# Cross attention on one core: V projected first, one head per period, K and V in one-bank blocks

## The chip, the cores and the metric
The kernel runs on one core of one Trainium2 chip. Its time is the device time of one launch in microseconds; one launch computes all 16 batches. All arithmetic is float32, and most matmuls split each operand into a high and a low part (float32r), so that one product becomes three: high x high, high x low, low x high.

## The reference
B = 16 batches, S = 100 rows of x with H = 640 features, 8 heads of D = 80, an encoder sequence of 718 rows (KEYS) with C = 384 features, and T = 4 further rows ca. Cut to what matters:

```python
query, keyt, valt = x @ Wq, enc @ Wk, enc @ Wv
hs = mha(query, keyt, valt)                        # softmax(Q K^T / sqrt(80)) V, 8 heads
ca_q1 = einsum('btc,th->bch', ca, Wq_ca)[:, indices, :]   # 100 of 384 rows
ca_hs1 = mha(ca_q1, x, x)
ca_hs2 = mha(ca_hs1 @ Wq, ca @ Wk_ca, ca @ Wv_ca)  # over 4 keys
out = (hs + ca_hs2) @ Wout + b_out + x
```

## The kernel before
`prepare` makes what depends on weights and x alone (Q of all batches, the small tables of the second attention) and writes it to DRAM. `attend` has the main stage, a loop over batches, and then the output projection over tiles of 128 rows. This case is about `attend`.

Each engine has its own program, an order written out by hand (`batch(i)` in each engine's block), and semaphores between them. Nothing is scheduled at run time: an instruction that waits holds everything behind it on its engine. Names of one batch's steps:

- `keys(b, f)`, line 887: one of five 128-feature tiles of K^T = Wk^T enc^T over all 718 columns, as two halves of 360 in two PSUM banks (`psS`, shared with the scores). ScalarE copies the high part (`k_high`, L1131), VectorE makes the low part (`k_low`, L1346).
- `lift` on SP, L674 and L677: DMAs that restack K^T from tiles of 128 features to heads of 80 rows, in `kstack`, 120 rows for two copies and the low parts, with four slots for heads.
- `scores(i, h)`, L864: four matmuls into `psS`. VectorE takes the row maximum (`rowmax`, L1322), ScalarE the exponential with its sum (`expo`, L1114), VectorE normalises (`norm`, L1327 and L1329).
- `turn(i, h)`, L901: six transpositions of P into `psT`; ScalarE `pt_high` (L1120), VectorE `pt_low` (L1335).
- `context(i, u)`, L918: U = enc^T P^T for four heads at once, 400 columns, one of three 128-feature tiles for each half of the heads; ScalarE `u_high` (L1149), VectorE `u_low` (L1351). It needs enc in its natural layout (`encN`), which is loaded and split besides `encT`: ScalarE L1143, GpSimd L812.
- `values(i, half)`, L941, L947, L948: Wv^T U per head, with the second attention's last product in the same accumulation.
- The second attention: `b2_scores` (L961), `b2_less_max` (VectorE, L1358 and L1360), `b2_exp`, `b2_norm` (VectorE, L1366, L1368, L1370), `b2_turn` (L971), `b2_values` (L984), `b2_scores2`, `b2_less_max2`, `b2_exp2`, `b2_norm2` (L1403 to L1407), and `b2_turn2` (L1007), one transposition of P2x per batch. GpSimd prepares its operands (`spread_g` L779 to L788, `split_x`).

Steps of three batches overlap: the contexts 2 to 5 and the values of a batch run in the next one, and the first three K tiles of the next batch run in this one. The output projection (`tile`, L1022, thirty matmuls of 320 columns) needs Wout split; ScalarE copies it (`wo_high`, L1181), GpSimd makes its low parts (L835).

Of the kernel before, what the change touches and what calls it, by code (L numbers as in the profile page):

```python
# [13 lines left out]
HEADS = 8  # L14
# [13 lines left out]
KT = 6  # L28
# [4 lines left out]
GT = 4 * S  # L33
STK = 3 * D // 2
# [45 lines left out]
def build(nc, x, xT, encT, encN, caT, asel, Wq, WqT, Wk, Wv, WqcaBD, Wkca, Wvca, Wout, bout, out):  # L80
# [6 lines left out]
    with ExitStack() as keep:  # L87
# [7 lines left out]
        Wo_s = [t[:, 0:FT * H].rearrange("p (c n) -> p c n", c=FT) for t in (wk_keep, eT_keep)]  # L95
# [3 lines left out]
        attend(nc, Wk_s, Wv_s, Wo_s, eT_s, ident, headmask, x, encT, encN, asel, Wout, bout,  # L99
# [392 lines left out]
def attend(nc, Wk_s, Wv_s, Wo_s, eT_s, ident, headmask, x, encT, encN, asel, Wout, bout,  # L492
# [6 lines left out]
    with ExitStack() as ctx:  # L499
# [9 lines left out]
        PRING = 3  # L509
        PARTS = CT  # L510
        KQ = KT // PARTS
        encT_raw, enc_raw = sb("encT_raw", [128, CT * KEYS]), sb("enc_raw", [128, KT * C])
        rawT = encT_raw[:, :].rearrange("p (c k) -> p c k", c=CT)
        rawN = enc_raw[0:KP, :].rearrange("p (k c) -> p k c", k=KT)
        eT = eT_s
        eN = pair("encN", [KP, KT, C])
        kT = [pair(f"kT{j}", [128, KEYS]) for j in range(2)]

        kst = sb("kstack", [STK, 2, SLOTS, KEYS], F32R)
        P = [sb(f"probs{j}", [128, KPAD]) for j in range(PRING)]  # L520
        PT = pair("PT", [KP, KT, R])
        UT = sb("UT", [128, CT, 4, 2, S], F32R)

        qst = pair("qstack", [STK, HEADS, S])
        hs = sb("hs", [D, RH])
        negmax, total, inv = sb("negmax", [S, HEADS]), sb("total", [S, HEADS]), sb("inv", [S, HEADS])

        xr, xs = sb("x_raw", [S, H]), pair("x", [S, H])
# [3 lines left out]
        v2 = sb("v2bd", [ST, H], F32R)  # L532
        Ms = sb("Min", [D, 2, HEADS, HEADS, T], F32R)
        P1 = sb("P1", [S, HEADS, S])
# [3 lines left out]
        P2T = sb("P2T", [ST, S], F32R)  # L538
        st1 = sb("st1", [S, 3, HEADS])
        st2 = sb("st2", [S, 3, HEADS])  # L540


        hs1T = [[PT[p][0:D, 0:4, (7 - half) * S:(8 - half) * S] for half in range(2)] for p in range(2)]

        psS = [ctx.enter_context(nc.psum_tensor(f"psS{j}", [128, 2, 512], F32)) for j in range(2)]
        psT = ctx.enter_context(nc.psum_tensor("psT", [128, 2, 512], F32))

        psB = ctx.enter_context(nc.psum_tensor("psB", [128, 2, 512], F32))


        loads = "rawT rawN qin gin ain xin v2in min woin0 woin1 bias hsout"

        products_done = "scores pt u kp hsp b2s b2t b2pv b2c b2t2 cmm"

        exps_and_highs = "exp pthi uhi khi hscopy b2exp p1hi hs1hi b2exp2 p2hi encThi encNhi wohi chi"

# [17 lines left out]
        score_slot = [0, 1, 1, 0, 0, 1, 0, 0]  # L574
# [1012 lines left out]
```

## Time and profile before
| | |
|---|---|
| three runs | 1098.77, 1101.1, 1110.14 us |
| median | 1101.1 us |
| profiled execution, first to last instruction | 1101.6 us |
| mean granted TensorE clock | 0.963 |
| first b2_turn2 to the last, 15 batches | 177.7 to 1019.8 us |

The profiled execution is given by its span alone; no other time of it is recorded. Read the table with the rows further down: times in them are microseconds from the start of the span, a duration in a group row is the mean of one instruction in ns, and TensorE's instructions overlap, so that the distance between two starts tells what one costs the stream.

### The profile page before, as it was taken

How to read it: one execution, taken by the hardware profiler on the slowest of the kernel's cores; microseconds unless marked ns; L12 is line 12 of the kernel's file. 1: busy time of each engine (PE TensorE's matmuls, PEld its weight loads, DVE VectorE, ACT ScalarE, POOL GpSimd, SP SyncE). 2: the span in 40 equal slices, each digit the busy share in tenths (PEclk: the TensorE clock that was granted, in tenths of full speed). 3: DMA queues.
4: the chain of work that ended last, by engine and by line, in shares of the span. 5: the costliest groups of instructions: out<-in, count | busy, mean ns of one | idle time of the engine just before them, and what ended most of it. 6: DMA issues, size and time to landing. Idle time of an engine off the chain costs nothing.

```text
span 1101.6 us, 21261 instructions
## 1 busy us (share of the span) xinstructions
PE 1036.2 (94%) x7192; PEld 1011.9 (92%) x7192; DVE 668.4 (61%) x1138; ACT 490.6 (45%) x889; POOL 280.9 (26%) x208
## 2 busy tenths in 40 slices
PE   6998759999989899999999998999999999998998
PEld 5997749999989899999999998999999999898997
DVE  4444356676756656576656674667675676666344
ACT  4443243635454535354545453455544454445110
POOL 0000132323231322323233323142433151415000
PEclk9899779999999999899999998999998999999999
DMA  8676786767887969596969694869695969697255
GB/s 303 219 204 154 166 173 153 182 163 187 170 171 148 196 133 202 119 211 139 193 142 212 138 196 112 207 148 208 145 198 112 206 152 195 142 200 184 66 172 160
DMA packets 155050, 189.51 MB, mean 172 GB/s; under 512 B 78416, under 2 KB 108112, under 8 KB 155024
## 3 DMA queue, kind: packets, MB, share of 16 engines
q1 hardware_dynamic: 151696, 181.63, 72.3%
q10 hardware_dynamic: 3328, 7.54, 2.1%
q8 instruction: 16, 0.26, 0.1%
q14 instruction: 10, 0.08, 0.0%
HBM read 81.15 MB, written 19.74 MB: 92 GB/s over the span
## 4 chain that ended last, share of the span: by engine, by line
PE 70%; DMA 11%; SPq 4%; DVE 2%; ACT 1%; issue 1%; POOL 0%; DVEq 0%; ACTq 0%; POOLq 0%
PE psB L918 23%; PE psS L887 20%; DMA kstack<-kT_l 10%; PE psS L864 6%; PE psT L901 5%; PE psS L1022 4%; PE psT L941 4%; PE psT L947 2%; SPq L677 2%; PE psB L984 2%; SPq L674 1%; PE psB L1002 1%; DVE kT_l L1346 1%; PE psB L996 1%; PE psT L948 1%
## 5 line engine op out<-in xcount | busy, mean ns | idle before, releaser
L887 PE MATMUL psS<-encT_keep,Wk_keep 128*128 128x360 f32 x1440 | 264.1, 338 | 5.9 <-PEq L173 5.3
L887 PEld LDWEIGHTS psS<-encT_keep,Wk_keep 128*128 128x128 f32 x1440 | 247.4, 196 | 6.7 <-issue 5.3
L918 PE MATMUL psB<-PT_h,encN_h 120*128 120x400 f32 x576 | 203.7, 354 | 0.2 <-POOL encN_l L812 0.2
L918 PE MATMUL psB<-PT_l,encN_h 120*128 120x400 f32 x576 | 199.4, 346 | 0.0
L918 PE MATMUL psB<-PT_h,encN_l 120*128 120x400 f32 x576 | 198.5, 345 | 0.0
L1114 ACT ACTIVATE probs<-psS,negmax 100x718 f32<-100x718 f32 x128 | 110.4, 863 | 169.9 <-DVE negmax L1322 146.6
L1346 DVE TENSOR_TENSOR kT_l<-psS,kT_h 128x718 fp32r<-128x718 f32 x80 | 72.4, 905 | 112.0 <-ACT kT_h L1131 111.9
L1131 ACT ACTIVATE kT_h<-psS 128x718 fp32r<-128x718 f32 x80 | 61.7, 771 | 146.9 <-PE psS L887 137.0
L804 POOL TENSOR_TENSOR encT_keep<-encT_raw,encT_keep 128x718 fp32r<-128x718 f32 x45 | 79.4, 1763 | 181.5 <-ACT encT_keep L1137 179.1
L864 PE MATMUL psS<-kstack,qstack_h 120*100 120x360 f32 x256 | 90.7, 354 | 32.8 <-DMA kstack<-kT_l 27.0
L812 POOL TENSOR_TENSOR encN_l<-enc_raw,encN_h 120x768 fp32r<-120x768 f32 x48 | 90.7, 1889 | 116.3 <-ACT encN_h L1143 115.0
L1322 DVE TENSOR_REDUCE negmax<-psS 100x1 f32<-100x720 f32 x128 | 113.6, 897 | 2.6 <-PE psS L864 2.5
L918 PEld LDWEIGHTS psB<-PT_h,encN_h 120*128 120x128 f32 x576 | 109.2, 190 | 1.5 <-POOL encN_l L812 0.8
L1335 DVE TENSOR_TENSOR PT_l<-psT,PT_h 120x600 fp32r<-120x600 f32 x128 | 99.7, 779 | 16.0 <-ACT PT_h L1120 10.8
L918 PEld LDWEIGHTS psB<-PT_l,encN_h 120*128 120x128 f32 x576 | 109.3, 190 | 0.0
L918 PEld LDWEIGHTS psB<-PT_h,encN_l 120*128 120x128 f32 x576 | 108.9, 189 | 0.0
L1351 DVE TENSOR_TENSOR UT<-psB,UT 128x400 fp32r<-128x400 f32 x96 | 55.0, 573 | 84.1 <-ACT UT L1149 84.1
L1329 DVE TENSOR_SCALAR probs<-probs,inv 100x718 f32<-100x718 f32 x128 | 103.0, 805 | 4.5
L901 PE MATMUL psT<-ident,probs 100*120 100x100 f32 x768 | 87.8, 250 | 8.6 <-DVE PT_l L1335 7.2
L1149 ACT ACTIVATE UT<-psB 128x400 fp32r<-128x400 f32 x96 | 48.4, 504 | 97.5 <-PE psB L918 97.3
L901 PEld LDWEIGHTS psT<-ident,probs 100*120 100x120 f32 x768 | 78.0, 137 | 15.0 <-issue 11.1
L795 POOL CAST x_h<-x_raw 100x640 fp32r<-100x640 f32 x16 | 14.2, 890 | 290.5 <-DMA x_raw<-in_x_dram 290.5
(143 smaller groups left out, 1868.4 us busy)
## 6 DMA issues: line engine op xcount, KB each, us to landing
kstack<-kT_h SPq DMA_DIRECT2D x64, 448.8 KB
kstack<-kT_l SPq DMA_DIRECT2D x192, 112.2 KB
enc_raw<-in_encN_dram SPq DMA_DIRECT2D x16, 1080.0 KB, 10.9
encT_raw<-in_encT_dram SPq DMA_DIRECT2D x15, 1077.0 KB, 8.5
kstack<-kT_h SPq DMA_DIRECT2D x32, 359.0 KB
kstack<-kT_h SPq DMA_DIRECT2D x32, 269.2 KB
kstack<-kT_h SPq DMA_DIRECT2D x32, 179.5 KB, 4.1
xT_raw<-in_xT_dram SPq DMA_DIRECT2D x4, 1000.0 KB, 7.8
```

The lines of the kernel that those rows point to most:

```text
L804: nc.gpsimd.tensor_tensor(eT[1][:, c, :], rawT[:, c, :], eT[0][:, c, :], ALU.subtract).then_inc(s["encT"], 1)
L812: nc.gpsimd.tensor_tensor(eN[1][:, ks, :], rawN[:, ks, :], eN[0][:, ks, :], ALU.subtract).then_inc(s["encN"], 1)
L864: mm = pe.matmul(psS[score_slot[h]][0:S, half, 0:HALF], qst[p][:, h, :], kst[:, p, h % SLOTS, k0:k0 + HALF], start=(p == 0), stop=(p == 1))
L887: mm = pe.matmul(keys_in(f, first)[:, half, 0:HALF], w[:, c, f * 128:(f + 1) * 128], e[:, c, k0:k0 + HALF], start=(j == 0), stop=(j == 3 * ...
L901: mm = pe.transpose(psT[0:KP, k // 3, (k % 3) * S:(k % 3 + 1) * S], P[h % PRING][0:S, k * KP:(k + 1) * KP], ident[0:S, 0:S])
L918: mm = pe.matmul(psB[:, 1, 0:RH], e[:, k, c * 128:(c + 1) * 128], a[:, k, half * RH:(half + 1) * RH], start=(j == 0), stop=(j == 3 * KT - 1))
L1114: nc.scalar.activation(halves(P[h % PRING][0:S, 0:KEYS]), without_overlap(psS[score_slot[h]], S), ACT.Exp, bias=negmax[:, h:h + 1], accum_ ...
L1131: nc.scalar.activation(halves(kT[f % 2][0][:, :]), without_overlap(keys_in(f, first), 128), ACT.Copy).then_inc(s["khi"], 1)
L1322: nc.vector.tensor_reduce(negmax[:, h:h + 1], tile_in(h), AX.XY, ALU.max, negate=True).then_inc(s["negmax"], 1)
L1329: nc.vector.tensor_scalar(P[h % PRING][0:S, 0:KEYS], P[h % PRING][0:S, 0:KEYS], inv[:, h:h + 1], None, ALU.mult).then_inc(s["norm"], 1)
L1335: nc.vector.tensor_tensor(o[1], psT[0:KP, :, 0:3 * S].rearrange("p a (k n) -> p a k n", k=3), o[0], ALU.subtract).then_inc(s["ptlo"], 1)
L1346: nc.vector.tensor_tensor(halves(kT[f % 2][1][:, :]), without_overlap(keys_in(f, first), 128), halves(kT[f % 2][0][:, :]), ALU.subtract).t ...
```

## The change
Three things go together.

1. V = enc Wv is made first, in twelve blocks ("v", columns, k) of up to 120 keys x 320 features, nine matmuls each, from `encT` and `Wv`. Then `values(i, j, h)` forms V^T P^T per head: six matmuls of 200 columns (high and low part of P^T side by side), six of 100, one for the second attention. `context` and its evictions go, and so do the load and the split of `encN`.
2. K is made in ten half tiles ("k", f, half), one bank each. K and V blocks, 22 a batch, alternate between the two banks of `psK`; block n waits for the low part of block n - 2. Scores have `psS` for themselves, one buffer: scores of a head wait for the exponential of the head before.
3. Each engine's batch is laid out in eight periods, one per head: scores, a block, the turn of the head before, a block, the values of the head before that, and often a third block. `OWN` and `NEXT` say which blocks a period has. The second attention runs one batch ahead, spread over the periods. `encT`, the values' small operands and PT have two buffers, and the loop body holds two batches.

On SP, q comes in two halves of heads and hs is stored in quarters. In the last batch Wout is loaded at the start, copied by ScalarE at the end of period 5, and its low parts are made by GpSimd after the last K block. The diff, cut to its core, SP first, then GpSimd's last batch, TensorE, ScalarE (exponential, period 0, end of period 5), VectorE (periods 0 to 4):

```diff
+BLOCKS = (("k", 0, 0), ("k", 0, 1), ("v", 0, 0),
+          ("k", 1, 0), ("k", 1, 1), ("v", 0, 1),
+          ("v", 0, 2), ("v", 0, 3), ("v", 0, 4),
+          ("k", 2, 0), ("k", 2, 1), ("v", 0, 5),
+          ("k", 3, 0), ("k", 3, 1), ("v", 1, 0),
+          ("v", 1, 1), ("v", 1, 2),
+          ("k", 4, 0), ("k", 4, 1), ("v", 1, 3),
+          ("v", 1, 4), ("v", 1, 5))
+NB = len(BLOCKS)
+AT = {what: n for n, what in enumerate(BLOCKS)}
+
+
+OWN = ((6, 7, 8), (9, 10, 11), (12, 13, 14), (15, 16), (17, 18, 19), (20, 21), (), ())
+NEXT = ((), (), (), (), (), (), (0, 1, 2), (3, 4, 5))
...
+                def batch(i, j, first=False, last=False):
+                    if not last:
+                        load_ga(i + 1)
+                        load_encT(i + 1)
+                        load_x(i + 1)
+                    else:
+                        load_wo()
+                    lift(i, 2)
                     if not first:
+                        store_hs(i - 1, 3)
                     lift(i, 3)
+                    if not last:
+                        load_q(i + 1, 0)
+                    else:
+                        for k in range(2):
+                            sp.wait_ge(s[f"hsout{k}"], 32 * (B - 1))
+                    store_hs(i, 0)
+                    if not last:
+                        load_m(i + 1)
                     lift(i, 4)
+                    if not last:
+                        load_v2(i + 1, 1 - j)
+                    else:
+                        for t in range(2):
+                            sp.wait_ge(s["wolo"], t + 1)
+                            load_tile(t)
+                    store_hs(i, 1)
                     if not last:
                         lift(i + 1, 0)
+                        load_q(i + 1, 1)
                         lift(i + 1, 1)
+                    store_hs(i, 2)
...
+                pool.wait_ge(s["bp"], NB * (B - 1) + AT["k", 4, 1] + 1)
...
+                def projected(b, j, n):
+
+                    what, f, half = BLOCKS[n]
+                    if n == 0:
+                        wait_pos(pe, s["encT"], CT * b)
+                    wait_pos(pe, s["blo"], NB * b + n - 1)
+                    m = 0
+                    if what == "k":
...
+                    else:
+                        cols, k = f, half
+                        for c in range(CT):
+                            for e, w in products(eT[j], Wv_s):
+                                mm = pe.matmul(psK[0:tiles_of(k), n % 2, 0:VH], e[:, c, k * KP:k * KP + tiles_of(k)],
+                                               w[:, c, cols * VH:(cols + 1) * VH], start=(m == 0), stop=(m == 3 * CT - 1))
+                                m += 1
+                    mm.then_inc(s["bp"], 1)
...
+                def values(i, j, h):
+
+                    pe.wait_ge(s["ptlo"], HEADS * i + h + 1)
+                    if h == 0:
...
+                    def high(k):
+                        n = tiles_of(k)
+                        return pe.matmul(both, V[0][0:n, k, hh], pt[0:n, k, :, :].rearrange("p a n -> p (a n)"),
+                                         start=(k == 0), stop=(k == KT - 1))
+
+                    def low(k):
+                        n = tiles_of(k)
+                        pe.matmul(o, V[1][0:n, k, hh], pt[0:n, k, 0, :], start=False, stop=False)
+
+                    for k in range(KT - 1):
+                        high(k)
+                        low(k)
+                    low(KT - 1)
+                    pe.matmul(o, v2[j][:, hh], P2T[j][:, :], start=False, stop=False)
+                    high(KT - 1).then_inc(s["pv"], 1)
...
+                    scores(i, 0)
+                    block(0, 0)
                     if not first:
+                        turn(i - 1, 7)
+                    block(0, 1)
                     if not first:
+                        values(i - 1, 1 - j, 6)
+                    b2_turn2(i)
+                    block(0, 2)
+
+                    scores(i, 1)
+                    block(1, 0)
+                    turn(i, 0)
+                    block(1, 1)
+                    if not first:
+                        values(i - 1, 1 - j, 7)
+                    block(1, 2)
+                    if not last:
+                        b2_scores(i + 1, 0)
+
                     scores(i, 2)
+                    block(2, 0)
+                    turn(i, 1)
+                    block(2, 1)
+                    values(i, j, 0)
+                    if not last:
+                        b2_scores(i + 1, 1)
+                    block(2, 2)
+
                     scores(i, 3)
+                    block(3, 0)
                     turn(i, 2)
+                    values(i, j, 1)
+                    block(3, 1)
+
                     scores(i, 4)
+                    if not last:
+                        b2_turn(i + 1, 0)
+                    block(4, 0)
+                    turn(i, 3)
+                    block(4, 1)
+                    values(i, j, 2)
+                    block(4, 2)
+
                     scores(i, 5)
+                    if not last:
+                        b2_turn(i + 1, 1)
+                    block(5, 0)
+                    turn(i, 4)
+                    values(i, j, 3)
+                    if not last:
+                        b2_values(i + 1, 0)
+                    block(5, 1)
+
                     scores(i, 6)
+                    block(6, 0)
+                    turn(i, 5)
+                    block(6, 1)
+                    if last:
+                        tile(0)
+                    values(i, j, 4)
+                    if not last:
+                        b2_values(i + 1, 1)
+                    block(6, 2)
+
                     scores(i, 7)
+                    block(7, 0)
                     turn(i, 6)
+                    if not last:
+                        b2_scores2(i + 1)
+                    block(7, 1)
+                    values(i, j, 5)
+                    block(7, 2)
+
+                b2_scores(0, 0)
+                projected(0, 0, 0)
                 b2_scores(0, 1)
+                projected(0, 0, 1)
+                projected(0, 0, 2)
+                projected(0, 0, 3)
+                b2_turn(0, 0)
+                projected(0, 0, 4)
+                b2_turn(0, 1)
+                projected(0, 0, 5)
+                b2_values(0, 0)
+                projected(0, 0, 6)
+                b2_values(0, 1)
+                projected(0, 0, 7)
+                projected(0, 0, 8)
+                b2_scores2(0)
...
+                def expo(i, h):
                     act.wait_ge(s["negmax"], HEADS * i + h + 1)
+                    wait_pos(act, s["pt"], HEADS * i + h - 1)
...
+                    expo(i, 0)
+                    block(0, 0)
                     if not first:
+                        pt_high(i - 1, 7)
+                    block(0, 1)
+                    b2_exp2(i)
+                    block(0, 2)
+                    b2_pt2_high(i, j)
...
+                    if not last:
+                        b2_hs_high(i + 1, 0)
+                    else:
+                        for c in range(FT):
+                            wo_high(c)
+                        tile_high(0)
...
+                    rowmax(i, 0)
+                    block(0, 0)
+                    norm(i, 0)
                     if not first:
+                        pt_low(i - 1, 7)
+                    block(0, 1)
+                    b2_norm2(i)
+                    block(0, 2)
+                    b2_pt2_low(i, j)
+
+                    rowmax(i, 1)
+                    block(1, 0)
+                    norm(i, 1)
+                    pt_low(i, 0)
+                    block(1, 1)
                     if not first:
+                        hs_add(i - 1, 3)
+                    block(1, 2)
+                    if not last:
+                        b2_less_max(i + 1, 0)
+
                     rowmax(i, 2)
+                    block(2, 0)
+                    norm(i, 2)
+                    pt_low(i, 1)
+                    block(2, 1)
+                    if not last:
+                        b2_less_max(i + 1, 1)
+                    block(2, 2)
+
                     rowmax(i, 3)
+                    block(3, 0)
                     norm(i, 3)
                     pt_low(i, 2)
+                    if not last:
+                        b2_norm(i + 1)
+                    hs_add(i, 0)
+                    block(3, 1)
+
                     rowmax(i, 4)
+                    block(4, 0)
+                    if not last:
+                        b2_pt_low(i + 1, 0)
+                    norm(i, 4)
+                    pt_low(i, 3)
+                    block(4, 1)
+                    block(4, 2)
```

## Rows read from the trace of the kernel before
**Rows 1.** The page, first part: busy us, share of the span, instructions.
```profile
PE 1036.2 (94%) x7192; PEld 1011.9 (92%) x7192; DVE 668.4 (61%) x1138; ACT 490.6 (45%) x889; POOL 280.9 (26%) x208
```
**Rows 2.** Windows cut at b2_turn2: busy by engine, granted clock, DMA share, GB/s.
```profile
109.70:177.70 68.00, 49.62 (x269) 46.54 (x270) 32.09 (x58) 23.73 (x43) 18.81 (x15) 0.76 0.74 156
...
572.00:625.20 53.20, 53.19 (x387) 52.34 (x386) 36.29 (x64) 27.03 (x51) 17.93 (x12) 1.00 0.77 176
625.20:686.70 61.50, 57.99 (x390) 56.80 (x388) 36.22 (x64) 27.51 (x51) 16.80 (x12) 0.92 0.75 156
...
907.10:963.10 56.00, 53.37 (x388) 52.65 (x387) 36.40 (x64) 27.34 (x51) 17.66 (x12) 1.00 0.81 170
...
1019.80:1101.60 81.80, 75.27 (x516) 74.19 (x513) 35.46 (x47) 12.42 (x21) 0.00 (x0) 1.00 0.43 133
```
**Rows 3.** The waits: engine, line, for whom, us in total, times, longest.
```profile
PE psS L864 <- DMA kstack<-kT_l: 27.0, 13, 4.4
```
**Rows 4.** TensorE's timeline in one batch and in the tail: start, us, form.
```profile
501.59 3.19 PE L887 MATMUL psS<-encT_keep,Wk_keep 128*128 128x360 f32 x18
504.61 0.68 PE L901 MATMUL psT<-ident,probs 100*120 100x100 f32 x6
505.07 0.39 PE L864 MATMUL psS<-kstack,qstack_h 120*100 120x360 f32 x1
...
518.36 0.35 PE L918 MATMUL psB<-PT_h,encN_h 120*128 120x400 f32 x1
...
521.63 0.33 PE L864 MATMUL psS<-kstack,qstack_h 120*100 120x360 f32 x1
...
529.87 0.46 PE L941 MATMUL psT<-UT,Wv_h 128*80 128x200 f32 x3
530.17 0.35 PE L947 MATMUL psT<-UT,Wv_l 128*80 128x100 f32 x3
530.36 0.24 PE L948 MATMUL psT<-P2T,v2bd 96*80 96x100 f32 x1
...
1025.52 0.31 PE L1022 MATMUL psS<-Wk_keep,kT_h 128*128 128x320 f32 x1
...
1029.94 0.35 PE L918 MATMUL psB<-PT_h,encN_h 120*128 120x400 f32 x1
```
**Rows 5.** Timeline of VectorE and ScalarE, a row maximum and what follows.
```profile
522.86 0.90 DVE L1322 TENSOR_REDUCE negmax<-psS 100x1 f32<-100x720 f32 x1
...
523.87 0.86 ACT L1114 ACTIVATE probs<-psS,negmax 100x718 f32<-100x718 f32 x1 [1.53 <-DVE negmax L1322]
...
524.88 0.87 ACT L1159 ACTIVATE P<-P 100x800 f32<-100x800 f32 x1
```
**Rows 6.** Groups by form: times | busy us, mean ns | idle before, released by.
```profile
L1329 DVE TENSOR_SCALAR probs<-probs,inv 100x718 f32<-100x718 f32 x128 | 103.0, 805 | 4.5
L1335 DVE TENSOR_TENSOR PT_l<-psT,PT_h 120x600 fp32r<-120x600 f32 x128 | 99.7, 779 | 16.0 <-ACT PT_h L1120 10.8
L1346 DVE TENSOR_TENSOR kT_l<-psS,kT_h 128x718 fp32r<-128x718 f32 x80 | 72.4, 905 | 112.0 <-ACT kT_h L1131 111.9
L1351 DVE TENSOR_TENSOR UT<-psB,UT 128x400 fp32r<-128x400 f32 x96 | 55.0, 573 | 84.1 <-ACT UT L1149 84.1
L1149 ACT ACTIVATE UT<-psB 128x400 fp32r<-128x400 f32 x96 | 48.4, 504 | 97.5 <-PE psB L918 97.3
L1370 DVE TENSOR_TENSOR P<-P,st 100x800 f32<-100x800 f32 x16 | 17.2, 1074 | 0.6
L1366 DVE TENSOR_REDUCE st<-P 100x8 f32<-100x800 f32 x16 | 15.7, 979 | 0.0
```
**Rows 7.** GpSimd: the last step of its first work, and the low parts of Wout.
```profile
114.28 0.39 POOL L788 TENSOR_TENSOR a<-a_raw,a 32x100 fp32r<-32x100 f32 x1
...
L835 POOL TENSOR_TENSOR encT_keep<-encT_raw,Wk_keep 128x640 fp32r<-128x640 f32 x5 | 8.2, 1638 | 11.0 <-ACT Wk_keep L1181 10.7
```
**Rows 8.** The lifts' issues on SP, from issue to landing.
```profile
DMA to landing us min/median/max: 2.9/4.3/8.5
```

More of the change, by code:

```diff
@@ L954, in b2_scores @@
+                def b2_scores(i, half):
                     if half == 0:
@@ new lines, in _ @@
+                b2_values(0, 1)
+                projected(0, 0, 7)
+                projected(0, 0, 8)
+                b2_scores2(0)
+                batch(0, 0, first=True)
+                with pe.Fori(0, (B - 2) // 2) as r:
+                    batch(2 * r + 1, 1)
+                    batch(2 * r + 2, 0)
+                batch(B - 1, 1, last=True)
+                tile(1)
+                turn(B - 1, 7)
+                values(B - 1, 1, 6)
+                tile(2)
+                values(B - 1, 1, 7)
@@ new lines, in _ @@
+                batch(0, 0, first=True)
+                with act.Fori(0, (B - 2) // 2) as r:
+                    batch(2 * r + 1, 1)
+                    batch(2 * r + 2, 0)
+                batch(B - 1, 1, last=True)
+                pt_high(B - 1, 7)
+                tile_high(2)
+                store(0)
+                load_x(2)
+                hs_copy(B - 1, 3)
+                for t in range(1, TILES):
+                    if t + 2 < TILES:
+                        tile_high(t + 2)
+                    store(t)
+                    if t + 2 < TILES:
+                        load_x(t + 2)
@@ L1506, in _ @@
+                    if not last:
+                        b2_less_max2(i + 1)
+                    hs_add(i, 2)
+                    block(7, 2)
+                for j in range(2):
+                    nc.vector.memset(P[j][:, KEYS:KPAD], 0.0).then_inc(s["ready"], 1)
                 b2_less_max(0, 0)
-                rowmax(0, 0)
+                low(0, 0)
                 b2_less_max(0, 1)
-                rowmax(0, 1)
-                batch(0, first=True)
-                with dve.Fori(1, B - 1) as i:
-                    batch(i)
@@ new lines, in _ @@
+                b2_pt_low(0, 0)
+                low(0, 4)
+                b2_pt_low(0, 1)
+                low(0, 5)
+                b2_hs_low(0, 0)
+                low(0, 6)
+                b2_hs_low(0, 1)
+                low(0, 7)
+                low(0, 8)
+                b2_less_max2(0)
+                batch(0, 0, first=True)
+                with dve.Fori(0, (B - 2) // 2) as r:
+                    batch(2 * r + 1, 1)
+                    batch(2 * r + 2, 0)
+                batch(B - 1, 1, last=True)
```

1014 lines of the change are left out of this document (401 added, 613 removed).

## The prediction
> **What bounds the kernel now.** I read the busy shares first: TensorE is busy 94% of the 1101.6 us, VectorE 61% [rows 1]. Then the main stage batch by batch, cut at the one transposition of P2 that every batch has. The windows show two kinds of batch: undisturbed ones of 53.2 us at full clock, in which TensorE is never idle, and ones of 56 to 61.5 us [rows 2]. What makes the difference is in the list of waits: TensorE waited 27.0 us in 13 places for a kstack transfer [rows 3], and after most of these the granted clock was at its lower level (1.2 of 2.4 GHz) for a while. In [rows 2] the batch of 61.5 us at clock 0.92 lost 61.5 x 0.08 = 4.9 us to that, the one of 56.0 us at clock 1.00 nothing; over the nine of fifteen such windows with a wait of over 1 us the loss, added up in this way, is 20.7 us, 2.3 on average. So the bound is TensorE's stream (15 batches of 53.2 = 798 us of the 842 us from the first such transposition to the last), and what can be won in the loop is 44 us of waits and low clock. The first batch is far worse: 68.0 us at clock 0.76 for less than a batch of work [rows 2]. The profiled execution's span, 1101.6 us, is 0.5 us over the median of the runs (1101.1), so I add up spans and take the sum as the median.
>
> **The TensorE work hardly changes.** Costs are distances between starts, since recorded matmuls overlap [rows 4]. A K tile of 18 matmuls of 360 columns takes 504.61 - 501.59 = 3.02 us (0.168 each), a transposed head 0.46, a context group of 18 x 400 columns 521.63 - 518.36 = 3.27, thirty matmuls of 320 columns 4.42 (0.147 each). In the values, three of 200 columns take 0.30 and three of 100 columns 0.19. Removed per batch: six context groups, 19.6 us, and both values steps, 8 heads x 0.56 = 4.5 us; together 24.1. Added: twelve V blocks of nine matmuls of 320 columns, 12 x 1.32 = 15.9 us, and eight heads of 6 x 0.10 + 6 x 0.063 + 0.07 = 1.05, 8.4 us; together 24.3. The alternation of 200 and 100 columns is in no row; from below the pair costs its columns (0.125), from above 0.172 (0.10 and the small matmul's 0.07): -0.2 to +0.06 us a head. I take 0.163, since both kinds are in the rows next to each other. K as ten half blocks of 1.51 us costs what five tiles did. The batch stays at 53.6 us of TensorE. The gain of the product order itself is nothing; all depends on the waits.
>
> **A rule that speaks against it.** The rows show a 360-column matmul every 0.168 us, 0.150 of which are its columns at 2.4 GHz, so a 128-column weight load is nearly hidden [rows 4]. The Trainium skill, TensorE: Matmul & The Clock Gate, sections LDWEIGHTS and The mechanism, has a load cost its columns at 1.2 GHz and overlap a running matmul only in another row group. The rows disagree with that. By it the change would load 21,280 columns of weights a batch in place of 18,304, some 2.5 us more; I leave it to the last rival.
>
> **What the new order asks of VectorE.** Each batch is now eight periods, and each period's order on VectorE is: row maximum, low part of block A, normalise, low part of P^T of the head before, low part of block B, something of the second attention, block C. Low A stands behind ScalarE's exponential of the same head, which stands behind the row maximum. From [rows 5]: maximum at 522.86, exponential at 523.87 (1.01 later), the next ScalarE instruction at 524.88 (1.01 later); with the block's high part, 0.504 for 400 columns and some 0.45 for 320 to 360 [rows 6], low A starts 2.5 us after the maximum started, and VectorE, busy for 0.82 of it, is idle 1.7 us in each of eight periods. That idle time is hidden while TensorE's period is longer than VectorE's. K and V evictions cost VectorE more too: ten of 360 and twelve of 320 columns. Between 573 ns at 400 and 905 at 718 columns [rows 6] the slope is 1.04 ns a column, so 0.53 and 0.49, or 0.45 and 0.41 where the next one follows (records overlap by 0.08): 9.4 us against 5 x 0.83 + 6 x 0.49 = 7.1 before. Four additions of hs in place of two cost about 0.3 more. Removed are the load and the splits of enc in its other layout, on ScalarE and GpSimd; nothing on the path of [rows 2]'s full-clock batches waited for them, so I count them at nothing.
>
> TensorE's periods by these prices: 0: 6.3; 1: 6.8; 2: 6.8; 3: 4.9; 4: 7.0; 5: 6.2; 6: 7.5; 7: 8.0 us. Periods 3 and 0 are where TensorE asks for something that the second attention makes on VectorE.
> *Wait A*, b2_turn of the next batch right after scores(4): from the start of scores(3) VectorE needs 0.66 (scores) + 0.2 (a matmul's end lies 501.59 + 3.19 - 504.61 = 0.17 behind the next start [rows 4]) + 2.5 + 0.41 (low A) + 0.93 (reciprocal and scaling, 0.805 on average [rows 6]) + 0.70 (P^T low) + 2.2 (b2_norm: 0.98 + 0.2 + 1.07 [rows 6]) = 7.6 us. TensorE is there after 0.66 + 1.32 + 0.56 + 1.05 + 1.32 + 0.66 = 5.6. It waits 2.0. VectorE also enters period 3 late: both b2_less_max passes (1.1 us each, two passes of 400 columns) stand at the end of periods 1 and 2, the first after a block low part that itself ends some 1.1 us into the next period. Followed through that is 0.9 us, so A is 2.0 to 3.0; I take 2.9. Queued behind b2_turn on TensorE are block 17, the turn of head 3 and everything else.
> *Wait B*, b2_turn2 in period 0: 0.66 + 0.2 + 2.5 + 0.41 + 0.93 + 0.70 + 0.41 (low B) + 0.75 (b2_norm2, three dependent short steps) = 6.6 us, against 0.66 + 1.32 + 0.56 + 1.32 + 1.05 = 4.9: 1.7 us.
> Elsewhere every block has its low part out of the way 1.4 us or more before its bank is wanted, and scores, turns and values want results of a period earlier.
>
> **The lifts.** Their number and bytes are the same. A lift lands 4.3 us after issue (median; 8.5 at most [rows 8]), and now each K tile is finished one and a half to two periods, about 9 us, before the first head that needs it. SP's queue gets four more q loads and two more hs stores; they stand between lifts, each in a gap of a period. The 27 us of waits and their low clock go. At scores(4) a landing can be up to 1 us late, in front of wait A, which covers it.
>
> **Clock.** A batch with waits lost 0 to 5.4 us before, 2.3 on average; now each batch has 4.6 us of waits in two places. I take 2.3, with 0 and 5.4 as ends.
> Batch period: 53.6 + 2.9 + 1.7 + 2.3 = 60.5 us, against (1019.8 - 177.7) / 15 = 56.1.
>
> **Ramp and tail.** TensorE's first instruction is now b2_scores, behind GpSimd's split of a, which ended at 114.67 [rows 7]; before, K started at 109.7. Then 12.9 us of blocks, 4.3 of the second attention, 2.7 for the cold clock, 2.5 waiting for b2_norm: scores(0,0) at 137.2, and after the chain of period 0 scores(0,1) at about 142.1, with no lift waits. From scores(15,1): 38.6 us of periods, of which nothing of the next batch is part; tiles 50.9; head 6, 7 and the last turn 2.7; the drain 4.6. In the last batch the split of Wout is queued on ScalarE at the end of period 5, and GpSimd's five low parts follow it at 1.64 us [rows 7] and 0.15 between them: 9 us, which the first output tile in period 6 waits out. I put that at 9.2 and 2.0 for the clock behind it. Together 108.0.
> Sum: 142.1 + 15 x 60.5 + 108.0 = 1157.6, say **1158 us**.
>
> **The rivals.**
> *TensorE-bound, faster.* The waits A and B don't form, the lift waits are gone, P is 54.2, the tail wait half hidden: 142.1 + 813 + 102 = 1057. For it: VectorE's busy time is only some 38 us a batch (36.3 to 37.2 busy before [rows 2], plus 2.6, less overlap), so on average there is room. Against: both waits come out of a chain in one queue, and no average fills it. It needs VectorE to be 2 us faster over one period; its longest single step there, the scaling at 0.805 [rows 6], would have to vanish, and more. Chance 0.12.
> *Waits without the clock.* A at 2.0, B 1.7, full clock after them as after the one of the 56.0 us batch, Wout hidden: P = 57.3, 142.1 + 859.5 + 97 = 1098.6: no change. Chance 0.14.
> *Low clock after every wait, slower still.* Its place is behind b2_turn in period 4 and behind b2_turn2: if TensorE's clock falls to 1.2 GHz at both in every batch, the loss is that of the worst window, 5.4 us, and P = 63.6: 1204. Chance 0.10.
> *Narrow weight loads not hidden.* If each of the twelve alternating matmuls of a head paid its load, about 0.06, it would be 0.76 a head, 6 us a batch, of which 1.5 only shorten A and B: 1158 + 15 x 4.5 = 1226. The skill's rule above has less, 2.5 us a batch: near 1195. Rows 4 speak against both. Chance 0.03.
> *It doesn't do what it says*: the lifts still hold scores because DMA queues are as full as before (0.77 to 0.81 busy [rows 2]). Each would cost 1 us where no other wait covers it; this only adds to my forecast, inside its range.
>
> **How the numbers follow.** The forecast itself has 0.61. The range reaches from 1095, just under the no-change case, to 1200: below it lies the faster rival, above it part of the last two. Faster by over 1% (under 1090) 0.13, within 1% 0.12, slower 0.75. One per cent, 11 us, is about what runs of this kernel can tell (they lie 11 us apart).
>
> **What would show it.** Each batch should have two idle places on TensorE: before the transpositions of P (b2_turn, released by VectorE's P normalisation), 2 to 3 us, and before the one of P2x, 1.7 us. kstack should be gone from the list of waits. Batches should be near 60 us, evenly, with clock 0.93 to 1.0; V blocks 1.32 us apart per nine. VectorE's low part of block A should start 2.5 us after the row maximum. The first output tile should wait some 9 us for GpSimd's split of Wout. I am wrong if TensorE reaches b2_turn later than VectorE's normalisation ends, or if the clock stays up after waits of 2 to 3 us.

## The result, and the profile after
| | before | after |
|---|---|---|
| median of four runs each, us | 1099.93 (1098.42 to 1110.14) | 1178.65 (1176.03 to 1179.59) |
| profiled execution: span | 1101.6 | 1174.0 |
| mean granted TensorE clock | 0.963 | 0.954 |

The ratio is 1.0675, 95% interval 1.0616 to 1.0733 (the two medians alone would give 1.072): the change makes the kernel slower by 6.8%. The forecast was 1158 us, range 1095 to 1200. Ratios, here and in the experiments, leave out slow runs, in which the granted clock was lower: some of the kernel before, more than 1.5% above its fastest run on the same chip, and one of experiment 5, 1673.9 us at clock 0.555.

The first part of the page after and its row of the granted clock, to be set against [rows 1]:

```profile
span 1174.0 us, 23696 instructions
## 1 busy us (share of the span) xinstructions
PE 1048.1 (89%) x7960; PEld 1023.8 (87%) x7960; DVE 695.9 (59%) x1345; ACT 490.1 (42%) x1049; POOL 179.6 (15%) x160
...
PEclk9997889899999999999989999999999999999799
```

TensorE is busy 12 us longer than before while the span grew by 72: 60 of the 72 are idle time of TensorE. The windows of after, cut as in [rows 2] at the one transposition of P2x that every batch has (columns: window, its length, busy by engine, clock, DMA share, GB/s). A common batch, one with a loop end in it, the only one at full clock, and the tail:

```profile
443.30:503.20 59.90, 55.44 (x434) 54.47 (x434) 38.14 (x77) 27.16 (x60) 10.90 (x9) 0.97 0.55 140
747.00:810.20 63.20, 57.14 (x433) 55.85 (x434) 38.31 (x77) 27.38 (x60) 10.93 (x10) 0.95 0.54 137
992.50:1050.70 58.20, 53.82 (x434) 52.87 (x435) 38.06 (x77) 26.93 (x60) 10.86 (x9) 1.00 0.58 147
1050.70:1174.00 123.30, 101.40 (x710) 99.86 (x710) 56.29 (x88) 30.80 (x60) 8.15 (x5) 0.91 0.51 146
```

The third row is the one to read: at full clock a batch has 53.8 us of TensorE work, 0.6 more than one before ([rows 2]: 53.20), and still takes 58.2. Where the 4.4 us are, and what else waits, is in the list of waits of after (for whom, us in total, times, longest), which answers to [rows 3]:

```profile
PE psB L942 <- DVE P L1381: 49.8, 16, 3.3
...
PE psB L978 <- DVE P2x L1418: 21.8, 16, 4.8
...
PE psS L858 <- issue: 11.5, 6, 2.3
...
PE psB L932 <- POOL a L799: 10.4, 1, 10.4
...
PE psK L996 <- POOL Wk_keep L843: 8.6, 1, 8.6
```

kstack, 27.0 us before, is gone from it: the high part of a lift lands 3.0 us after its issue (median, 3.3 at most), against 4.3 and 8.5 [rows 8]. L942 is b2_turn in period 4 (wait A), L978 is b2_turn2 in period 0 (wait B). L858 is the first scores of every second batch. L996 is the first output tile. L932 is b2_scores, TensorE's first instruction here.

Wait A on TensorE, first the start of scores(3) and then b2_turn (start, duration, form, idle time before):

```profile
458.29 0.32 PE L858 MATMUL psS<-kstack,qstack_h 120*100 120x360 f32 x1
...
467.18 0.55 PE L942 MATMUL psB<-ident,P 100*100 100x100 f32 x4 [3.18 <-DVE P L1381]
```

The chain in front of it on VectorE, from the row maximum of head 3 to the end of b2_norm:

```profile
459.57 0.90 DVE L1330 TENSOR_REDUCE negmax<-psS 100x1 f32<-100x720 f32 x1
461.81 0.49 DVE L1362 TENSOR_TENSOR V_l<-psK,V_h 120x320 fp32r<-120x320 f32 x1 [1.35 <-ACT V_h L1145]
462.22 0.15 DVE L1335 RECIPROCAL inv<-total 100x1 f32<-100x1 f32 x1
462.41 0.59 DVE L1337 TENSOR_SCALAR probs<-probs,inv 100x718 f32<-100x718 f32 x1
462.92 0.78 DVE L1343 TENSOR_TENSOR PT<-psT,PT 120x600 fp32r<-120x600 f32 x1
463.61 0.97 DVE L1377 TENSOR_REDUCE st<-P 100x8 f32<-100x800 f32 x1
464.62 0.20 DVE L1379 RECIPROCAL st<-st 100x8 f32<-100x8 f32 x1
464.86 2.27 DVE L1381 TENSOR_TENSOR P<-P,st 100x800 f32<-100x800 f32 x1
```

and GpSimd's row in the same time:

```profile
464.58 1.70 POOL L814 TENSOR_TENSOR encT_keep<-encT_raw,encT_keep 128x718 fp32r<-128x718 f32 x1 [5.38 <-ACT encT_keep L1151]
```

TensorE reaches b2_turn at 467.18 - 3.18 = 464.00, 5.71 us after scores(3) started (forecast 5.6). VectorE is 0.39 us into the first of b2_norm's three steps then. The last of them took 2.27 us where 1.07 was allowed: over all sixteen the median is 2272 ns and the least 991. (The 1074 ns of [rows 6] is itself a mean: before, the median was 992 and the longest 1467.) GpSimd's low part of encT had started 0.28 us earlier and ended at 466.28. If VectorE's step could do its work only from there, it would end at 466.28 + 0.99 = 467.27; it ended at 467.13. The Trainium skill says as much (SBUF — State Buffer, Who interferes with whom): a VectorE instruction with both inputs in SBUF and a GpSimd instruction that reads SBUF share a port pair, and the second fully blocks until the first is through. P and st both lie in SBUF, and GpSimd's step reads SBUF; the trace agrees to 0.14 us.

What the clock did behind this wait is in four windows: three in a row from the end of wait A, and one from the end of wait B (shown below) in the same batch:

```profile
467.18:469.00 1.82, 1.82 (x12) 1.82 (x13) 1.43 (x3) 0.35 (x1) 0.00 (x0) 0.86 0.45 111
469.00:471.00 2.00, 2.00 (x11) 1.92 (x10) 0.71 (x2) 1.67 (x5) 0.00 (x0) 0.50 0.29 82
471.00:473.00 2.00, 2.00 (x14) 1.99 (x12) 1.66 (x4) 0.58 (x2) 0.00 (x0) 0.77 0.00 0
...
503.15:506.00 2.85, 2.85 (x19) 2.85 (x20) 0.66 (x2) 0.57 (x2) 0.43 (x1) 1.00 0.24 45
```

Behind wait A TensorE works at 1.2 GHz for a while, which costs 0.14 x 1.82 + 0.50 x 2.00 + 0.23 x 2.00 = 1.7 us; behind wait B it stays at 2.4 GHz.

Wait B, and the wait at the end of the loop body:

```profile
503.15 0.29 PE L978 MATMUL psB<-ident,P2x 100*96 100x100 f32 x1 [1.28 <-DVE P2x L1418]
```

```profile
437.08 0.40 PE L858 MATMUL psS<-kstack,qstack_h 120*100 120x360 f32 x1 [1.65 <-issue]
```

"issue" means that nothing the profile shows held TensorE. It occurs six times, at each return to the start of the loop body, which now holds two batches. The queue that brings instructions moved 76 packets:

```profile
q8 instruction: 76, 1.25, 0.4%
```

against 16 before. In the tail two output tiles stand still for long, the first for GpSimd's Wout, the third for the low part of its hs tile:

```profile
1091.57 0.60 PE L996 MATMUL psK<-encT_keep,kT_h 128*128 128x320 f32 x1 [8.63 <-POOL Wk_keep L843]
```

```profile
1113.44 0.64 PE L996 MATMUL psK<-encT_keep,kT_h 128*128 128x320 f32 x1 [5.00 <-DVE kT_l L1432]
```

### The profile page after: what moved, and what is told of

It reads as the page before. It is cut to its first block, busy times and chain, and to the rows that moved or that the text cites. A ratio compares the mean times of both kernels' runs of the same rounds, so it can differ in the third digit from the quotient of the medians.

```text
span 1174.0 us, 23696 instructions
## 1 busy us (share of the span) xinstructions
PE 1048.1 (89%) x7960; PEld 1023.8 (87%) x7960; DVE 695.9 (59%) x1345; ACT 490.1 (42%) x1049; POOL 179.6 (15%) x160
## 3 DMA queue, kind: packets, MB, share of 16 engines
q8 instruction: 76, 1.25, 0.4%
## 4 chain that ended last, share of the span: by engine, by line
PE 60%; DVE 18%; issue 8%; ACT 3%; POOL 1%; DMA 1%; ACTq 0%; DVEq 0%; SPq 0%; POOLq 0%
PE psK L873 18%; PE psK L880 14%; PE psH L910 5%; PE psS L858 4%; PE psT L890 4%; DVE negmax L1330 3%; DVE P L1381 3%; PE psK L996 3%; DVE PT L1343 3%; PE psB L955 2%; DVE V_l L1362 2%; PE psH L915 2%; PE psS L996 2%; ACT V_h L1145 2%; PE psB L942 2%
## 5 line engine op out<-in xcount | busy, mean ns | idle before, releaser
L910 PE MATMUL psH<-PT,V_h 120*80 120x200 f32 (+1 forms) x768 | 155.2, 279 | 0.0
L873 PE MATMUL psK<-encT_keep,Wk_keep 128*128 128x360 f32 x720 | 148.2, 354 | 0.0
L880 PE MATMUL psK<-Wv_h,encT_odd 128*120 128x320 f32 (+1 forms) x576 | 147.3, 318 | 0.0
L873 PE MATMUL psK<-encT_odd,Wk_keep 128*128 128x360 f32 x720 | 145.5, 350 | 0.0
L880 PE MATMUL psK<-Wv_h,encT_keep 128*120 128x320 f32 (+1 forms) x576 | 145.4, 315 | 0.0
L873 PEld LDWEIGHTS psK<-encT_keep,Wk_keep 128*128 128x128 f32 x720 | 130.5, 207 | 0.1
L873 PEld LDWEIGHTS psK<-encT_odd,Wk_keep 128*128 128x128 f32 x720 | 128.0, 203 | 0.1
L915 PE MATMUL psH<-PT,V_l 120*80 120x100 f32 (+1 forms) x768 | 120.2, 214 | 0.0
L910 PEld LDWEIGHTS psH<-PT,V_h 120*80 120x80 f32 (+1 forms) x768 | 114.2, 149 | 0.0
L915 PEld LDWEIGHTS psH<-PT,V_l 120*80 120x80 f32 (+1 forms) x768 | 108.9, 151 | 1.1
L858 PE MATMUL psS<-kstack,qstack_h 120*100 120x360 f32 x256 | 85.2, 333 | 11.5 <-issue 11.5
```

Source lines behind the costliest of these rows:

```text
L858: mm = pe.matmul(psS[0:S, half, 0:HALF], qst[p][:, h, :], kst[:, p, h % SLOTS, k0:k0 + HALF], start=(p == 0), stop=(p == 1))
L873: mm = pe.matmul(psK[:, n % 2, 0:HALF], w[:, c, f * 128:(f + 1) * 128], e[:, c, k0:k0 + HALF], start=(m == 0), stop=(m == 3 * CT - 1))
L880: mm = pe.matmul(psK[0:tiles_of(k), n % 2, 0:VH], e[:, c, k * KP:k * KP + tiles_of(k)], w[:, c, cols * VH:(cols + 1) * VH], start=(m == 0) ...
L910: return pe.matmul(both, V[0][0:n, k, hh], pt[0:n, k, :, :].rearrange("p a n -> p (a n)"), start=(k == 0), stop=(k == KT - 1))
L915: pe.matmul(o, V[1][0:n, k, hh], pt[0:n, k, 0, :], start=False, stop=False)
```

## The experiments
**Theory**: the product order costs nothing; the loss is waits A and B, which come out of the order of VectorE's work, and the low clock behind them; wait A is 1.2 us longer because GpSimd works beside b2_norm. **Rivals**: the stream of V blocks and alternating values matmuls is itself dearer, or keeps the clock down; or what is taken out of one wait appears in the next. Each experiment is the changed kernel with the edit shown. Ratios are against the kernel before on the same chip; the median of its runs that count was 1087.8 us for the first four experiments, 1100.9 for the next four and 1095.6 for the last (of all its runs 1104.2, 1105.5 and 1104.4; they lie between 1086 and 1120). Gains in us are against the 1178.65 of the changed kernel, which was not run again beside the experiments. They are not exact to a few us, so each is set beside the waits and batch lengths of the traces, which repeat to about 0.2 us (a batch with both waits, no loop end and clock 0.97: 59.6 to 59.9 us in the changed kernel, 59.7 to 59.8 in experiment 5).

**1. TensorE asks later at both places.** ScalarE's and VectorE's copies of b2_turn move along.

```diff
-                    b2_turn2(i)
                     block(0, 2)
+                    b2_turn2(i)
...
                     scores(i, 4)
-                    if not last:
-                        b2_turn(i + 1, 0)
                     block(4, 0)
                     turn(i, 3)
+                    if not last:
+                        b2_turn(i + 1, 0)
```

> Against the changed kernel: b2_turn(i+1, 0) moved behind the turn of head 3 in period 4 (with its high and low parts on ScalarE and VectorE), b2_turn2 moved behind the third block of period 0. Theory (the two waits of 3.2 and 1.3 us a batch come from VectorE's in-order chain being asked too early): both go, the clock stays up, a batch falls from 60.8 to 54 to 54.5 us, the time from 1178 to about 1080 (1070 to 1095). Rival 1 (VectorE or the one-bank blocks are the bound, and moving the question only moves the wait): the batch stays at 58 us or more, the time above 1140. Rival 2 (the clock falls because of the many small matmuls, not because of the waits): waits go, the clock stays at 0.95 to 0.97, the batch is 56, the time about 1105.

Measured 1120.4 us, ratio 1.028 [1.017, 1.038]: 58 us less than the changed kernel, and still 25 over the 1095 that was the upper end of my expectation. Wait B is gone, A is not (VectorE's row and TensorE's, one batch):

```profile
331.38 2.29 DVE L1381 TENSOR_TENSOR P<-P,st 100x800 f32<-100x800 f32 x1
```

```profile
333.73 0.55 PE L942 MATMUL psB<-ident,P 100*100 100x100 f32 x4 [1.19 <-DVE P L1381]
```

The move is worth 1.9 us (block(4, 0) and a turn) and A had 3.18, so 1.3 had to stay, for which the expectation left too little room; what stays is as long as what GpSimd adds to b2_norm. Short batches took 55.7 us at clock 1.00. TensorE's busy time in such a batch is 54.4, 0.9 more than in experiment 2. Some 0.6 of that is waiting, hidden because the modelled end of a matmul lies behind the start of the next. From the start of the turn to b2_turn it takes 1.41 us longer than in experiment 7, of which 1.19 count as idle. And the block behind b2_turn starts 0.67 us after it in place of 0.28, since it needs the bank of block 16, whose low part stands behind b2_norm on VectorE:

```profile
333.87 0.47 DVE L1362 TENSOR_TENSOR V_l<-psK,V_h 120x320 fp32r<-120x320 f32 x1
...
334.40 0.63 PEld L873 LDWEIGHTS psK<-encT_odd,Wk_keep 128*128 128x128 f32 x4 [0.32 <-DVE V_l L1362]
```

So a small part of wait A did come up at a block, as the first rival of the expectation had it; the other 0.3 us stay open.

**2. Only wait A, from VectorE's side.** ScalarE makes b2_exp at the end of period 2, VectorE b2_norm right behind the row maximum of head 3, where it was idle for the exponential.

```diff
                     block(2, 2)
+                    if not last:
+                        b2_exp(i + 1)
...
                     rowmax(i, 3)
+                    if not last:
+                        b2_norm(i + 1)
                     block(3, 0)
                     norm(i, 3)
                     pt_low(i, 2)
-                    if not last:
-                        b2_norm(i + 1)
```

> TensorE's order as changed; ScalarE's b2_exp moved to the end of period 2 and VectorE's b2_norm directly behind the row maximum of head 3, into the time in which VectorE waits for the exponential. Theory: wait A goes (3.2 us and about 1.7 us of low clock a batch), wait B stays: a batch of 56 to 57 us, the time 1105 to 1125. Rival 1 (VectorE has no time left over, bound by its total): block A's low part is late by as much and the next block waits: no gain, above 1160.

Measured 1105.8 us, ratio 1.015 [1.004, 1.027], 73 less than the changed kernel, near the lower end of the expectation. A is gone, B stays (1.28 each). All sixteen b2_norm steps take 991 to 993 ns now, since they no longer coincide with GpSimd. A batch without a loop end:

```profile
306.40:361.20 54.80, 53.55 (x433) 52.91 (x433) 37.65 (x77) 26.91 (x60) 10.94 (x9) 1.00 0.59 150
```

54.80 - 1.25 = 53.55: the batch is the TensorE work and wait B, at full clock, although B is still there. The edit takes away both parts of A at once, the chain and GpSimd's; experiment 4 tells them apart.

**3. Only wait B.** `b2_turn2` behind `block(0, 2)`, the first half of the diff of experiment 1.

> Only b2_turn2 moved behind the third block of period 0. Theory: wait B (1.3 us a batch) goes, A stays at 3.2: 15 x 1.3 = 19 us less, and little of the low clock, since that follows A: 1150 to 1160. Rival 1: the wait moves to A or to a block, no gain (1175 to 1180). Rival 2 (B alone costs clock as well): 1130 to 1145.

Measured 1159.3 us, ratio 1.064 [1.051, 1.076], 19 less than the changed kernel. B is gone from the list of waits, A is as it was (50.2 us in 16 places), clock 0.957. Of B's 21.8 us 17.6 are gone (the first, 4.2, stays), and the gain is 19.3 by the medians, 15.7 by the profiled spans (1174.0 - 1158.3): B brought hardly any low clock, and nothing came up elsewhere. The ratio alone, 1.064 against 1.0675, could not tell this gain from none.

**4. Only GpSimd away from b2_norm.** The second and third high parts of encT, which GpSimd's low parts follow, go to periods 4 and 5.

```diff
                     block(3, 1)
-                    if not last:
-                        encT_high(i + 1, 1 - j, 1)
...
                     if not last:
-                        encT_high(i + 1, 1 - j, 2)
+                        encT_high(i + 1, 1 - j, 1)
...
                     hs_copy(i, 1)
+                    if not last:
+                        encT_high(i + 1, 1 - j, 2)
```

> The second and third copy of encT on ScalarE moved from the end of period 3 to period 4 and from period 4 to period 5, and with them GpSimd's low parts, so that none of them runs beside VectorE's last step of b2_norm (P times 1/sum, two operands in SBUF), which took 2.27 us in the changed kernel and 1.07 on average before. Theory (1.2 of the 3.2 us of wait A are GpSimd's): A falls to 2.0 us, 18 us less and perhaps some low clock: 1145 to 1162. Rival (the step is slow for another reason, or another step is slowed instead): no change, 1172 to 1182.

Measured 1156.1 us, ratio 1.059 [1.048, 1.070], 22.5 less. The same two instructions as in experiment 1, now:

```profile
335.87 0.99 DVE L1381 TENSOR_TENSOR P<-P,st 100x800 f32<-100x800 f32 x1
```

```profile
336.92 0.55 PE L942 MATMUL psB<-ident,P 100*100 100x100 f32 x4 [1.90 <-DVE P L1381]
```

2.27 became 0.99 and 3.18 became 1.90, both by 1.28: GpSimd's share of A is shown, and what stays is the forecast's 2.0. The wait of 1.90 us still brings low clock: thirteen of the fifteen batches lie below 1.00, twelve of them at 0.96 or 0.97.

**5. The loop end.** The batch loop of all five engines written out, nothing else.

```diff
-                with pe.Fori(0, (B - 2) // 2) as r:
+                for r in range((B - 2) // 2):
                     batch(2 * r + 1, 1)
```

> The changed kernel with its batch loops unrolled on all engines; nothing else. TensorE has a wait that the forecast did not have: 1.7 to 2.3 us before scores(i, 0) at six of seven loop ends, released by nothing the trace shows. Theory (it is the jump back to the top of a loop body of two batches, whose instructions have to be fetched anew): without the jump the waits go, 11.5 us and some low clock less: 1150 to 1168. Rival (the instructions have to be fetched in any case, as they are read once each now): the waits stay or spread, 1172 to 1190.

Measured 1159.2 us (median of three runs), ratio 1.056 [1.046, 1.066]. The six waits for "issue" are gone, and all batches but the first take 59.7 to 59.8 us. They cost 16.5 us of span (1174.0 - 1157.5) with 11.5 of waiting. The instruction queue still moved 64 packets, so it is not the number of packets that stops TensorE but the jump back to the start of the body; that the start must then be fetched again is argued, not shown.

**6. The tail.** Wout's high parts in periods 1 and 3 of the last batch (period 1 is shown), and on SP the bias load ahead of the last hs stores.

```diff
                     block(1, 2)
+                    if last:
+                        wo_high(0)
+                        wo_high(1)
...
-                        for c in range(FT):
-                            wo_high(c)
                         tile_high(0)
```

> Only the last batch: ScalarE copies Wout in periods 1 and 3 in place of the end of period 5, and the bias is loaded as soon as its slot is free. Theory (the first output tile's 8.6 us and the third's 5.0 us come from GpSimd's low parts starting late and from the bias queued behind all of them): the first wait falls to 0 to 4 us, the third tile's to under 3: 8 to 14 us less, 1163 to 1171. Rival (the tiles' own loads of hs, queued behind the last lift, take their place): at most 4 us less.

Measured 1176.7 us, ratio 1.069 [1.061, 1.077]: no gain beyond what runs can tell, so my expectation missed and its rival held. The first tile now waits for its own hs tile (the low part, L1432 of the changed kernel, is L1440 here), and so does the third. In front of the first stands ScalarE's split of that tile, waiting for the transfer of hs:

```profile
1091.48 0.74 ACT L1204 ACTIVATE kT_h<-encT_raw 128x640 fp32r<-128x640 f32 x1 [5.32 <-DMA encT_raw<-hs_all]
...
1093.13 0.64 PE L1000 MATMUL psK<-encT_keep,kT_h 128*128 128x320 f32 x1 [5.21 <-DVE kT_l L1440]
...
1113.35 0.63 PE L1000 MATMUL psK<-encT_keep,kT_h 128*128 128x320 f32 x1 [3.24 <-DVE kT_l L1440]
```

8.63 became 5.21 and 5.00 became 3.24, yet the tail went from 123.3 to 120.6 only; 0.84 us of waiting for a lift came up at the last scores.

**7. Waits A and B both gone.** Experiments 2 and 3 together.

> b2_norm early on VectorE (as alone before, 1105 us) and b2_turn2 behind the third block of period 0 (as alone before, 1159 us). Theory: waits A and B are the whole loss of the loop besides the loop's end, a batch is 53.6 us without and 56.5 with a loop end, mean 54.9 (from 56.0): 1084 to 1092. Rival (VectorE becomes the bound once both are gone): a new wait of 0.5 us or more a batch in another period, above 1096.

Measured 1086.9 us, ratio 0.989 [0.982, 0.996]. The rival of the expectation, a new wait on VectorE, did not come. This also decides between the theory and the rivals ahead of the experiments. A batch with a loop end, and one without:

```profile
247.90:303.70 55.80, 54.09 (x435) 52.97 (x434) 37.88 (x77) 26.89 (x60) 11.10 (x9) 1.00 0.62 156
303.70:357.30 53.60, 53.60 (x435) 52.76 (x434) 37.71 (x77) 26.89 (x60) 10.93 (x9) 1.00 0.61 154
```

In the second TensorE is busy in all of its 53.60 us, at full clock, with the same V blocks and the same alternating values: 53.6 was the forecast's figure for TensorE's work, and 53.2 that of a batch before. The stream neither costs more nor lowers the clock. The six loop ends stay; the first row has one.

**8. With the tail, and two K blocks ahead of the first b2_scores.** Experiments 7 and 6, and this (VectorE's low parts of the two blocks move along):

```diff
-                b2_scores(0, 0)
                 projected(0, 0, 0)
-                b2_scores(0, 1)
                 projected(0, 0, 1)
+                b2_scores(0, 0)
                 projected(0, 0, 2)
+                b2_scores(0, 1)
```

> The same with Wout's copies early, the bias early, and in the prologue the first two K blocks ahead of the second attention's first scores, which waited 10.4 us for GpSimd. Theory: 8 to 14 us less for the tail and 4 to 6 for the start: 1066 to 1076, 2 to 3% below the kernel before. Rival (the chain of the second attention sets the start, not its first product): 1076 to 1082.

Measured 1081.1 us, ratio 0.983 [0.977, 0.988]; the rival held. TensorE starts at 105.97 in place of 111.02, but b2_turn2 of the first batch at 137.0 in place of 139.3. Ahead of it TensorE still waits 2.99 us for VectorE's P and 4.53 for its P2x: the second attention's chain over VectorE and ScalarE sets that start, not the first blocks.

**9. The same with its loops written out.**

> All the edits of the version before this (both waits, tail, prologue), with the batch loops unrolled. The loop ends cost it six waits of 1.8 to 2.5 us and with the clock behind them 57.6 - 53.6 = 3.5 us each on average. Theory: all batches 53.5 to 53.9 us, 18 to 24 us less than with loops, 1056 to 1064. Rival (with a faster stream the fetch of instructions read once each becomes a wait of its own): 1068 or more.

Measured 1057.0 us, ratio 0.967 [0.960, 0.974]: 3.3% under the kernel before. Every batch between the first and the last is now like this:

```profile
190.50:244.00 53.50, 53.50 (x435) 52.90 (x434) 36.78 (x78) 26.93 (x60) 11.30 (x9) 1.00 0.63 157
```

## Why the prediction was right or wrong
The direction, and the mechanism that carries most of the loss, were right; several terms were mis-sized or missing, and some of the errors offset each other. The sum was 142.1 + 15 x 60.5 + 108.0 = 1157.6, measured 138.8 + 15 x 60.89 + 121.9 = 1174.0 (scores(0,1) started at 138.76, scores(15,1) at 1052.14). The range held the result; the forecast itself lies 20 us below it, most of that in the tail.

- **TensorE's work, 53.6 us a batch**: right, by experiments 7 (53.6) and 9 (53.4 to 53.5). The prediction's own terms give 53.2 - 24.1 + 24.3 = 53.4; it doesn't say where its 0.2 more come from. V blocks take 1.32 us, a head's values 1.06 (forecast 1.05), the pair of 200 and 100 columns 0.165 (0.163). The rule that speaks against it in the prediction fails: a pair and a head cost what was forecast without any weight load.
- **Wait A, 2.9 us**: measured 3.18 in the loop, but by another sum. The chain alone gives 1.90 (experiment 4; forecast 2.0). The step that failed is "Followed through that is 0.9 us": VectorE started the row maximum 459.57 - 458.29 = 1.28 us after scores(3) against the 0.86 allowed, so it was 0.4 late, and the steps behind it gave that back (low A 2.24 us behind the maximum, not 2.5; the scaling 0.59, not 0.805). The rest is b2_norm's last step beside GpSimd, 1.28 us, which no row of before had shown for this place and I had not put in. That the size came out nearly right is luck: 0.9 us that were not there stand for 1.28 that were missing. (Both sums, of A and of B, also put the turn at 0.56 us, where the prediction's own price and the traces have 0.46.)
- **Wait B, 1.7 us**: 1.28 in batches without a loop end, 0.6 to 1.1 in those with one, 1.1 on average.
- **The lifts**: right, their 27.0 us are gone.
- **Clock, 2.3 us a batch**: right in size: the length of each window times its missing share of the clock adds up to 36 us over the fifteen, 2.4 each. It was charged to both waits, but belongs to A and the loop end. Taking B away gained 19.3 us for 17.6 of waits (experiment 3); taking A away gained 72.9 for 47.8 (49.8 less 2.0, experiment 2), and batches with B alone have clock 1.00. The two gains add up: 92.2 against 91.8 for both (experiment 7). So A carried about 25 us of low clock, 1.7 a batch, as much as the three windows behind wait A show. The clock need not fall behind A: in the batch from 992.5, with the same 3.18 us, it stayed at 1.00, and no run here shows why.
- **The loop end**: missing. The sum has eight periods a batch and nothing for the jump back of a body that now holds two batches; it cost 11.5 us of waits, 16.5 with the clock. Per batch: A 0.3 over, B 0.6 under, TensorE's work 0.1 under, loop end 0.8 and clock 0.1 over make +0.5, where 60.9 - 60.5 = 0.4 was measured.
- **Ramp**: 138.8 against 142.1, 3.3 too much. TensorE's first instruction, behind GpSimd's split of a, started at 111.02, not at the 114.67 taken from before.
- **Tail, 108.0 us**: the largest miss, 13.9 us. The named term was right: the first tile waited 8.63 us where 9.2 stood. What failed is that the other tiles were taken as free: 5.00 and 3.14 us for hs tiles and 0.49 for an exponential, 8.6 us not in the sum. Then the clock: it falls behind three of these waits, here behind the first,

```profile
1090.00:1095.00 5.00, 3.43 (x13) 3.46 (x14) 3.05 (x6) 2.14 (x4) 1.47 (x1) 0.50 0.01 3
```

and TensorE's busy time times the missing share of the clock, added up in windows of 2 us, is 5.9 us, where 2.0 was allowed. 8.6 + 3.9 - 0.6 is 11.9 of the 13.9. The 2 us left are TensorE work: thirteen tiles at 4.42 are 57.5 us, not 50.9, while the 38.6 us of periods still hold some 4.1 of the next batch's second attention, 2.5 net. Experiment 6 shows that removing the named wait alone gives little: behind it stand the transfers and splits of hs.

Of the rivals, *waits without the clock* fell, as the clock did fall; so did *low clock after every wait*: it would have needed 5.4 us a batch, and 2.4 were lost. *Narrow weight loads* fell by the pair's 0.165, and the last, lifts that still hold scores, by their absence from the waits. *TensorE-bound* did not happen here, but the time it named, 1057, is that of the same products once both waits, the loop end and part of the tail are out of the way (experiment 9: 1057.0). That the two numbers agree is luck: it added 142.1 + 813 + 102, and the span of experiment 9 is 134.0 + 803.3 + 118.1, cut at b2_turn2.

Open: 0.3 us of TensorE time in a batch of experiment 1; what exactly is fetched at the loop end; and why the clock stays up behind wait A in one batch and falls in the others.

## What to carry to other kernels
A re-laid schedule is judged by the longest chain through one in-order queue up to each point at which the bound engine asks, not by that engine's average room: here VectorE was busy in 38 of 60 us, and one step moved ahead in its queue (and its exponential in ScalarE's) was worth 73 us. For each step of such a chain look at what GpSimd does in the same microsecond if both read SBUF. When a loop body doubles, look at its end in the trace, and when a wait in the tail is priced, price the one behind it too.

## What the runs showed of the hardware
- A VectorE multiplication of 100 x 800 with both inputs in SBUF took 0.99 us alone and 2.27 beside a GpSimd step of 1.70 that had started 0.28 earlier; moving GpSimd's step brought back 0.99 (experiment 4), and took 1.28 us off TensorE's wait.
- The end of a loop body of two batches, some 870 matmuls with as many weight loads, cost TensorE 1.65 to 2.3 us each time, up to 2.9 in experiment 4, and nothing when written out (experiment 5).
- One wait of 1.28 us in a batch left the granted clock at its full 2.4 GHz (1.00 in experiment 2). With one of 1.90 us as well most batches had 0.97 (experiment 4), with one of 3.18 in its place most had 0.94 to 0.97 (the changed kernel). Behind the wait of 3.18 the clock went down to 1.2 GHz for some us, but in one batch of fifteen it didn't.
